# Four 64x64 tiles of TensorE for the entering states of a two-way Mamba-2 layer, states kept without zeros, and engine orders written anew

## The reference

```
zxbcdt = x @ Win                       # z 512, xBC 640, dt 8
xBC = silu(causal_conv4(xBC) + convb)  # xs 512 = 8 heads x 64, B 64, C 64
dt = softplus(dt + dtb); dA = exp(dt * -exp(Alog))
h_t = dA_t * h_(t-1) + dt_t * x_t B_t^T    # one state of 64 x 64 for each head
y_t = C_t h_t + D * xs
out = rmsnorm(y * silu(z)) * normw @ Wout
```

## Time and profile before

| | |
|---|---|
| median of three runs | 636.88 us (635.69 to 637.5) |
| profiled execution | 635.01 us |
| its span | 633.2 us |
| PE busy | 602.9 us, 95% of the span |
| ACT busy | 545.8 us, 86% |
| DVE busy | 510.0 us, 81% |
| POOL busy | 363.1 us, 57% |
| mean granted clock of TensorE | 0.997 |

### The profile page before, as it was taken

One profiled execution on the slowest core, in us unless ns is written; L12 is line 12 of the kernel. 1 busy time (PEld: TensorE's weight loads), 2 busy tenths in 40 slices (PEclk: granted clock), 3 DMA queues, 4 the chain that ended last, 5 costly groups with the idle time before them and its releaser, 6 DMA issues.

```text
span 633.2 us, 13301 instructions
## 1 busy us (share of the span) xinstructions
PE 602.9 (95%) x3996; PEld 492.4 (78%) x3996; DVE 510.0 (81%) x1056; ACT 545.8 (86%) x1220; POOL 363.1 (57%) x367
## 2 busy tenths in 40 slices
PE   2998999999999999999999999999999999999995
PEld 1676788887888878887888878888788878888784
DVE  3779788986979689797888869798797978788663
ACT  4799998979997998979989799889989799897862
POOL 1026656666575664765556675656647665465933
PEclk9999999999999999999999999999999999999998
DMA  7552614245160632407132361505416071332600
GB/s 223 158 180 92 208 23 132 57 119 192 25 184 0 193 116 65 144 9 248 51 126 83 98 211 25 182 3 177 131 29 180 1 217 59 101 111 67 211 1 33
DMA packets 43544, 70.70 MB, mean 112 GB/s; under 512 B 8000, under 2 KB 30592, under 8 KB 43520
## 3 DMA queue, kind: packets, MB, share of 16 engines
q1 hardware_dynamic: 43520, 70.40, 36.5%
HBM read 59.37 MB, written 4.72 MB: 101 GB/s over the span
## 4 chain that ended last, share of the span: by engine, by line
PE 80%; ACT 9%; DVE 5%; issue 3%; POOL 2%; DMA 0%; SPq 0%; POOLq 0%; ACTq 0%; DVEq 0%
PE mi L612 17%; PE pj L485 9%; PE py L578 9%; PE pj L487 9%; PE pj L486 9%; PE py L590 6%; PE mi L565 4%; PE mi L678 3%; PE mi L545 2%; PE mi L598 2%; ACT bs L964 2%; ACT L952 1%; DVE xdt L1418 1%; POOL xw L1906 1%; PE mi L671 1%
## 5 line engine op out<-in xcount | busy, mean ns | idle before, releaser
L1406 DVE SCALAR_TENSOR_TENSOR xc<-pj,cw,xc 128x509 f32<-128x509 f32 (+2 forms) x240 | 173.9, 742 | 20.5 <-ACT xc L934 19.1
L964 ACT ACTIVATE bs<-bs,s_all 128x128 f32<-128x128 f32 x512 | 159.3, 392 | 0.0
L1929 POOL TENSOR_TENSOR yg<-yg,sz 128x512 f32<-128x512 f32 x60 | 76.6, 1287 | 87.3 <-DVE yg L1455 87.3
L485 PE MATMUL pj<-xnt_hi,w_hi 128*128 128x512 f32 x288 | 121.2, 421 | 3.8 <-DVE xnt_lo L1323 2.9
L487 PE MATMUL pj<-xnt_hi,w_lo 128*128 128x512 f32 x288 | 114.1, 396 | 0.0
L486 PE MATMUL pj<-xnt_lo,w_hi 128*128 128x512 f32 x288 | 113.9, 395 | 0.0
L612 PE MATMUL mi<-wc,yg 128*128 128x256 f32 x480 | 110.9, 384 | 0.0
L612 PEld LDWEIGHTS mi<-wc,yg 128*128 128x128 f32 x480 | 88.7, 190 | 14.0 <-issue 3.2
L1937 POOL TENSOR_TENSOR sqsum<-sqsum,sq 128x512 f32<-128x512 f32 x45 | 57.9, 1287 | 60.7 <-ACT sq L984 60.0
L1433 DVE TENSOR_TENSOR bs<-bs,gm 128x512 f32<-128x512 f32 x128 | 85.9, 676 | 6.7 <-ACT bs L970 6.3
L1906 POOL TENSOR_TENSOR xw<-xdt,w_end 128x512 f32<-128x512 f32 x48 | 49.7, 1044 | 48.7 <-DVE xdt L1418 37.5
(11 more groups left out here) (151 smaller groups left out, 1040.3 us busy)
## 6 DMA issues: line engine op xcount, KB each, us to landing
bs<-rows_dram SPq DMA_DIRECT2D x64, 512.0 KB, 5.0
es<-rows_dram SPq DMA_DIRECT2D x128, 96.0 KB, 3.3
cc<-bcm SPq DMA_DIRECT2D x32, 128.0 KB, 3.1
xres<-in_x SPq DMA_DIRECT2D x8, 512.0 KB, 3.8
out<-ot SPq DMA_DIRECT2D x32, 128.0 KB, 3.7
xin<-in_x SPq DMA_DIRECT2D x7, 512.0 KB, 4.1
cz<-bcm SPq DMA_DIRECT2D x16, 128.0 KB, 3.4
rows_dram<-s_rows SPq DMA_DIRECT2D x128, 4.0 KB
```

Source lines behind the costliest of these rows:

```text
L485: pe.matmul(ps[:], hi(k), xnt_hi[:, k, :], start=(k == 0), stop=False)
L964: i = nc.scalar.activation(bs[:, h, Q * c:Q * c + Q], bs[:, h, Q * c:Q * c + Q], ACT.Relu, bias=s_all[:, d, 0, c, h:h + 1], scale=-1.0)
L1406: i = dve.scalar_tensor_tensor(xc[:, t, to], pj[bank][:, of], cw[:, d, t, KW - 1 - s:KW - s], xc[:, t, to], ALU.mult, ALU.add)
L1929: pool.tensor_tensor(yg[:, d, p, :], yg[:, d, p, :], sz[:, d, p, :], ALU.mult).then_inc(yg_ready, 1)
```

## The change

- **`inter` takes two pairs at a time.** It is called twice for a unit, not four times. For each of 3 chunks it issues four matmuls of 64 rows and 64 columns: the states of pair 2*two straight (rows 0 to 63 to columns 0 to 63, rows 64 to 127 to columns 64 to 127, into one `py` bank) and those of pair 2*two + 1 crossed (rows 0 to 63 to columns 64 to 127, rows 64 to 127 to columns 0 to 63, into the other bank). It waits until the `es` of both pairs is ready, and fills both banks before either is released.
- **States without zeros.** `hst` and `hs` have 64 columns for each pair. Odd pairs keep their two heads in swapped lanes (`MEMBERS`), and so do `es` and `e_end`. DVE's `state` is one instruction of 128 lanes, POOL's `decayed_state` multiplies 128 x 256 elements, `decay_e` is two instructions of ACT, one for each half of the lanes; `hst` isn't cleared.
- **Orders.** The lists of SP, PE, ACT, DVE and POOL in all five functions, and the order of uses of the `mi` banks, are written anew. In `forward_scan` and `reversed_scan` of PE both `intra` of two pairs stand ahead of their common `inter`, with projections or mixes between some of them.

```diff
-        e_end = sb("e_end", [P, 2, NCH])
+        e_end = sb("e_end", [P, 2, NC, KI])
-        hst = sb("hst", [P, NC - 1, KI, P])
-        hs = sb("hs", [P, KI, P])
+        hst = sb("hst", [P, NC - 1, KI, HP])
+        hs = sb("hs", [P, KI, HP])
+        LANES = [slice(0, HP), slice(HP, P)]
+        MEMBERS = [slice(0, 4, 3), slice(1, 3)]
...
-                    sp.dma_start(es[HP * e2:HP * e2 + HP, p, LATER[d]],
-                                 rows_dram[d, 1, 2 * p + e2, LATER[d]].partition_broadcast(HP)).then_inc(es_loaded[p], 16)
+                    sp.dma_start(es[LANES[e2], p, LATER[d]],
+                                 rows_dram[d, 1, 2 * p + (e2 ^ (p % 2)), LATER[d]].partition_broadcast(HP)).then_inc(es_loaded[p], 16)
...
-            def inter(phase, it, b, d, p):
+            def inter(phase, it, b, d, two):
                 u = 2 * b + d
-                bank, used = py_use(b, d, p)
-                if p == 0:
+                pairs = (2 * two, 2 * two + 1)
+                bank = [py_use(b, d, p)[0] for p in pairs]
+                if two == 0:
                     released(phase, it, f"{d}s{NC - 2}")
-                pe.wait_ge(c2_ready, 2 + KI * u + p + 1)
+                pe.wait_ge(c2_ready, 2 + KI * u + 2 * two + 2)
+                alone(pe)
                 for j in range(NC - 1):
                     c = ORDER[d][j + 1]
-                    mm = pe.matmul(py[bank][:, Q * c:Q * c + Q], hst[:, j, p, :], es[:, p, Q * c:Q * c + Q],
-                                   start=False, stop=(j == NC - 2), skip_group_check=True)
-                mm.then_inc(py_full[bank], 1)
+                    chunk = slice(Q * c, Q * c + Q)
+                    for swap in range(2):
+                        for half in range(2):
+                            rows, to = LANES[half], LANES[half ^ swap]
+                            mm = pe.matmul(py[bank[swap]][to, chunk], hst[rows, j, pairs[swap], :], es[rows, pairs[swap], chunk],
+                                           start=False, stop=(j == NC - 2), skip_group_check=True)
+                        if j == NC - 2:
+                            mm.then_inc(py_full[bank[swap]], 1)
...
             def reversed_scan(phase, it, b, nxt):
                 more = phase == "loop"
+                project(b, 1, NT - 1)
                 b_tokens(phase, it, b, 1)
                 x_tokens(phase, it, b, 1, 0)
-                project(b, 1, NT - 1)
...
                 state(phase, it, b, 1, 0)
+                state(phase, it, b, 1, 1)
                 wait_xnt(phase, it)
-                state(phase, it, b, 1, 1)
                 project(nxt, 0, 0)
...
+                intra(b, 1, 0)
                 state(phase, it, b, 1, 2)
-                intra(b, 1, 0)
                 intra(b, 1, 1)
+                project(nxt, 0, 3)
                 mix(phase, it, b, 0, 2)
+                inter(phase, it, b, 1, 0)
                 mix(phase, it, b, 0, 3)
-                inter(phase, it, b, 1, 0)
                 sums(phase, it, nxt, 0)
+                intra(b, 1, 2)
+                project(nxt, 0, 4)
+                intra(b, 1, 3)
+                s_transposed(phase, it, nxt, 0)
                 inter(phase, it, b, 1, 1)
-                project(nxt, 0, 3)
-                project(nxt, 0, 4)
-                intra(b, 1, 2)
-                s_transposed(phase, it, nxt, 0)
-                inter(phase, it, b, 1, 2)
-                intra(b, 1, 3)
-                inter(phase, it, b, 1, 3)
                 project(nxt, 0, 5)
...
             def forward_scan(phase, it, b, last):
...
                 project(b, 1, 0)
+                x_tokens(phase, it, b, 0, 3)
                 state(phase, it, b, 0, 0)
-                x_tokens(phase, it, b, 0, 3)
...
                 intra(b, 0, 0)
                 mix(phase, it, last, 1, 0)
                 mix(phase, it, last, 1, 1)
+                intra(b, 0, 1)
                 inter(phase, it, b, 0, 0)
                 mix(phase, it, last, 1, 2)
                 mix(phase, it, last, 1, 3)
                 sums(phase, it, b, 1)
                 project(b, 1, 3)
                 project(b, 1, 4)
-                intra(b, 0, 1)
                 s_transposed(phase, it, b, 1)
-                inter(phase, it, b, 0, 1)
+                intra(b, 0, 2)
                 norm2_transposed(phase, it, last, 0)
-                intra(b, 0, 2)
-                inter(phase, it, b, 0, 2)
+                intra(b, 0, 3)
                 norm2_transposed(phase, it, last, 1)
                 feed(phase, it, 0)
                 feed(phase, it, 1)
                 norm2_transposed(phase, it, last, 2)
-                intra(b, 0, 3)
+                inter(phase, it, b, 0, 1)
                 norm2_transposed(phase, it, last, 3)
-                inter(phase, it, b, 0, 3)
...
             def decay_e(b, d):
-                nc.scalar.activation(e_end[:, d], s_all[:, d, 1].rearrange("p c h -> p (c h)"), ACT.Exp).then_inc(end_ready, 1)
+                for half in range(2):
+                    ends = s_all[LANES[half], d, 1].rearrange("p c (s z) -> p c s z", z=4)[:, :, :, MEMBERS[half]]
+                    i = nc.scalar.activation(e_end[LANES[half], d].rearrange("p c (s z) -> p c s z", z=2), ends, ACT.Exp)
+                i.then_inc(end_ready, 1)
...
-                for half in range(2):
-                    lanes, cols = slice(HP * half, HP * half + HP), slice(HP * half, HP * half + HP)
-                    if j == 0:
-                        i = dve.tensor_copy(hst[lanes, j, :, cols], view[lanes])
-                    else:
-                        i = dve.tensor_tensor(hst[lanes, j, :, cols], view[lanes], hs[lanes, :, cols], ALU.add)
-                i.then_inc(free, 1)
+                if j == 0:
+                    dve.tensor_copy(hst[:, j], view).then_inc(free, 1)
+                else:
+                    dve.tensor_tensor(hst[:, j], view, hs[:], ALU.add).then_inc(free, 1)
...
-                pool.tensor_tensor(hs[:].rearrange("p r (e q) -> p (r e) q", e=2),
-                                   hst[:, j - 1].rearrange("p r (e q) -> p (r e) q", e=2),
-                                   e_end[:, d, o:o + NH].unsqueeze(2).broadcast_to([P, NH, HP]), ALU.mult).then_inc(hs_ready, 1)
+                pool.tensor_tensor(hs[:], hst[:, j - 1], e_end[:, d, ORDER[d][j], :].unsqueeze(2).broadcast_to([P, KI, HP]),
+                                   ALU.mult).then_inc(hs_ready, 1)
```

555 lines of the change are left out of this document (275 added, 280 removed).

## The result

The median of four runs of the changed kernel is 631.13 us (630.43 to 633.48), beside 636.97 us (635.69 to 637.5) for the kernel before; the ratio is 0.9921, with a 95% interval of 0.9906 to 0.9936. The forecast was 623.0 us: the sign is right and the time lies in the range, but the gain is 5.8 us where 13.9 were forecast. The profiled execution is the longest of the four, 633.48 us, span 631.6; the spans of the others are 628.6 to 629.4. Its mean granted clock is 0.989, theirs 0.995, 0.995 and 0.997. With a lower level of half the full clock that makes 13.9 us at the lower level in the profiled one and, as an estimate, 4 to 6 us in the others.

A forecast was written before the change was run, and what follows sets the result against it. PE, busy 95% of the span, was taken as the bound. Profiled: 635.0 - 21.9 + 9.3 - 3.2 + 0.9 + 1.0 = 621.1 us, so a median of 623; own range 618 to 629, with inside rivals 612 to 637.

The forecast's parts named there:

- -21.9 for inter: PE's inter matmuls: four 64 x 64 tiles run at once in 0.109 us, 42.8 us becoming 20.9.
- Rivals 1 and 2: In inter, row halves don't run side by side (chance 0.10), or PE can't issue that densely (0.05); median 644 either way.
- +9.3 for the shapes: PE's changes of tile shape: 1.19 us a turn, 8.3 for seven turns, 1.0 in the last scan.
- Rival 4: Entering and leaving 64 x 64 shape costs 0.43 us more per inter call, eating all; half gives 630; chance 0.08.
- States costless on PE: State work saved on DVE (20 us) and POOL (16), +3.4 on ACT, lies beside PE's work.
- -3.2 for the orders: New lists in the turn cover waits at forward state 0 and reversed state 1, 0.46 us a turn, seven turns.
- the same shortage exists now, so I add nothing: Reversed scan: moved projection no longer covers DVE's 0.69 us per xdt against PE's 0.44; counted as zero.
- +0.9 for two pairs coming out at once: At the end, DVE does outputs and gates of two pairs in 2.9 us instead of 2.0 for one.
- The lists of the opening move work by a place or two; I see no sum in them: Lists of SP, POOL and the opening: no term in the sum, 2 us either way in the range.
- +1.0 for ScalarE: ACT, busy 92% of a turn instead of 89%, shows its short waits somewhat more: +1 us.
- Rival 3: ACT becomes the bound: at 89.4% use a turn needs 74.9 us, time near 636, half 630; chance 0.07.

The follow-up runs named there:

- The 2 x 2 table: Turn times: 128 x 128 tiles 74.5 us in old orders, 75.3 in new; joined 64 x 64 tiles 76.7 in old orders, 73.1 in new.
- the edit meant for it: ScalarE's first reversed-scan bound put behind xnt_hi, against the run with VectorE's x_tokens evictions at half columns (626.98 us): 647.87 us.
- the last run: ScalarE's first reversed-scan bound put behind xnt_hi, against the run with reversed-scan intra of pairs 2 and 3 side by side (626.65 us): 647.65 us.

## Why the prediction was right and wrong

- **-21.9 for inter: right in the mechanism, 0.8 us too much.** 768 instructions, four at once, a slot of 0.109 us. 384 x 0.111 is 42.6, not 42.8, and the slots saved, 2.64 us for two units, are 21.1 for sixteen. Rivals 1 and 2 are out: 24 instructions in six slots are 0.027 us for each pair of load and matmul. The Trainium skill (TensorE: Matmul & The Clock Gate, Back-to-back issue gap) has 62 ns as the bound with hardware decode off; the trace shows less than half of that, so it isn't the bound here.
- **+9.3 for the shapes: right.** 0.14 to 0.17 into the 64 x 64 tiles and 0.18 to 0.20 out, 0.14 from half-width into them; 1.2 us a turn, as worked out. Rival 4 is out.
- **States costless on PE: right** in the turn (waits of 1.9 us with pairs apart and no zeros, 2.3 before). GpSimd's `hs` takes 0.616 us, not 0.55.
- **-3.2 for the orders: wrong**, by about 3.8 us. The waits named did go, but the sum of waits went from 2.3 to 2.4 us a turn. Here the reasoning "the same shortage exists now, so I add nothing" failed: project ahead of the x_tokens opened 1.38 us of waits where 1.13 stood, and more turned up at dt_transposed and the first norm2_transposed (0.2 and 0.3). The 2 x 2 table shows what the orders are for: they carry the joined step.
- **The last scan: wrong, by about 5 us.** The forecast gave it -1.3 of slots, +1.0 of shapes and +0.9 for two pairs coming out at once, so 41.7 us, and put its rewritten list at nothing. It took 46.8 in the profiled execution. Waits ahead of its first mixes grew from 0.2 to 3.1 us, and the clock was at the lower level for 13.6 us instead of 3.4, worth about 3 us. The +0.9 at the end can't be seen: the sums behind the last joined step wait 0.25 us longer, ScalarE's `xn` behind them 0.3 less. Priced by the runs, joining costs about 5 us in this stage: pairs apart bring the scan from 46.0 to 42.3 us, or from 44.7 to 41.2, each with 1.3 more of slots.
- **"The lists of the opening move work by a place or two; I see no sum in them": wrong.** Waits there grew by 3.5 us, the slower clock of its first 20 us included; the old opening gives about 1.7 of it back. The rest was not taken apart.
- **+1.0 for ScalarE:** not seen as a term of its own. The new wait at the first norm2_transposed is one for ScalarE (0.3 us a turn), that at dt_transposed went when its decay was halved (0.2); both are counted with the orders above. Rival 3 did not hold either in its form: with 3.3 us less of ScalarE's work in a turn (64.1 after 67.4 busy; the expectation had 5) it gets only 0.2 us shorter, although any delay of ScalarE at the wrong place costs its own length and more.

The seven turns came out at 73.1 for 72.6 forecast, 3.7 us of the miss; the two ends make the rest. Of the 5.7 us of the last scan some 1.9 are a first fall of the clock behind the waits at its start (the run with the old opening has the same list, no such fall and 44.9 us). A second, behind the last mixes, lasts 10.2 us where the kernel before has 3.4; instructions at twice their slot cost 2.7 us there and 1.3 before, so 1.4 more:

```profile
592.20:596.20 4.00, 3.66 (x12) 2.41 (x12) 1.46 (x5) 3.94 (x12) 3.37 (x5) 0.62 0.24 79
617.10:627.30 10.20, 6.92 (x20) 4.67 (x19) 5.11 (x18) 3.40 (x8) 4.24 (x7) 0.50 0.04 13
```

What sets the length of these falls wasn't tested. The three shorter executions, whose spans are 2.2 to 3.0 us shorter, weren't profiled; by their mean clock they had 8 to 10 us less at the lower level. What holds the turn at 73 us isn't one engine: every edit that delayed one of the chains cost 0.5 to 4 us a turn in the mean, and none that shortened one gave more than 0.2. That two chains end together at state 0 is shown by what each waits for; that shortening both would gain was not shown, since the edit meant for it delayed ScalarE.

## What to carry to other kernels

A step that is joined with its neighbour to fill the array saves slots at once, but its inputs and its results come due together; price it by what the other engines do between them, and keep it apart where nothing else can be put around it, as in the last stage. When a tuned list is rewritten, don't count old waits as won: list for each moved call what it covered on every engine (here a bound that covered a wait of ScalarE), since that wait comes back. Here 64 x 64 tiles paid four at a time, and cost time two at a time.

## What the runs showed of the hardware

- 64 x 64 tiles of float32 run four at a time at the slot of one 128 x 128 matmul, 0.109 us for 128 columns, with two PSUM banks and crossed quarters.
- A change of tile shape cost 0.14 us into 64 x 64 tiles and 0.20 us back to 128 x 128, by distance of ends.
- A wait of 1.5 to 1.6 us of TensorE between stretches of full work was followed by a granted clock of 0.50 for 3.4 us or more in four of seven turns of the last run; the first, fifth and seventh, with the same wait, kept the full clock. At the lower level 256 columns took 0.427 us instead of 0.216, and 3.4 us of it made a turn 1.5 to 1.7 us longer.
